# Delta inputs of a four-part kernel: scans at the end of VectorE's step, decay projected last, sums of squares in column tiles

## The reference, cut to what matters

```python
q = silu(silu(short_conv(h @ Wq, conv_q)))
k = silu(silu(short_conv(h @ Wk, conv_k)))
v = silu(short_conv(h @ Wv, conv_v))
beta, gamma = sigmoid(h @ Wb), sigmoid(h @ Wdec)
mix = sigmoid(silu(short_conv(h @ Wmix, conv_mix)) + mix_bias)
# q, k divided by sqrt(sum of squares per head + 1e-6), 4 heads of 64 columns
ema[t] = gamma[t] * ema[t-1] + (1 - gamma[t]) * v[t]      # a scan over the rows
# and, per chunk of 32 rows, the products k @ k.T that the delta rule inverts
```

## Time and profile before

| | |
|---|---|
| median of 3 runs | 1427.38 us (1426.36 to 1428.32) |
| the profiled execution's own time | 1430.96 us |
| its span (first to last instruction) | 1429.3 us |
| mean granted TensorE clock | 0.919 of full |
| busy in the span | PE 1274.9, DVE 822.0, POOL 497.4, ACT 463.4 us |
| `delta_inputs` in the trace | from about 621 to 913 us |

### The profile page before, as it was taken

The page is one execution under the profiler, slowest core; times in us unless marked ns, Lnnn a source line. Parts: engine busy times, 40 slices in busy tenths (PEclk is TensorE's granted clock), DMA queues, the critical chain, the costliest instruction groups (busy, mean ns, idle before and its releaser), DMA issues. The chain is left out here.

```text
span 1429.3 us, 36337 instructions
## 1 busy us (share of the span) xinstructions
PE 1274.9 (89%) x12853; PEld 951.0 (67%) x12854; DVE 822.0 (58%) x1882; ACT 463.4 (32%) x1085; POOL 497.4 (35%) x711
## 2 busy tenths in 40 slices
PE   6999999899999999927889787498999999889997
PEld 5888888767777777614555454387888888646564
DVE  5778888633222222238789887357566666435443
ACT  1211112132222222217667776112222222123332
POOL 3334666414511111064665642223343444210000
PEclk9999999989999999968878888559999999779999
DMA  9999910112321111121454433712643335000001
GB/s 313 351 369 341 330 44 35 36 51 100 118 64 59 59 59 59 52 77 52 141 142 128 123 89 94 195 50 74 111 108 95 95 94 149 7 1 30 30 22 37
DMA packets 219962, 156.60 MB, mean 110 GB/s; under 512 B 111744, under 2 KB 201344, under 8 KB 219840
## 3 DMA queue, kind: packets, MB, share of 16 engines
q1 hardware_dynamic: 210528, 129.51, 30.9%
q0 software_dynamic: 9312, 25.44, 5.3%
HBM read 64.47 MB, written 90.44 MB: 108 GB/s over the span
## 5 line engine op out<-in xcount | busy, mean ns | idle before, releaser
L945 PE MATMUL ps_sc<-w,a_qeo 128*128 x568 | 183.3, 466 | 0.0
L753 DVE TENSOR_TENSOR a_stm<-a_vpad,ps_sc 128x352 f32<-128x352 f32 x71 | 37.0, 521 | 177.3 <-ACT a_vpad L517 156.6
L945 PEld LDWEIGHTS ps_sc<-w,a_qeo 128*128 128x128 f32 x568 | 104.1, 193 | 46.5 <-issue 2.5
L423 POOL DMA_DIRECT2D x_slots<-a_stm x66 | 36.5, 552 | 226.1 <-issue 226.1
L1583 PE MATMUL d_pp<-d_xT,d_w_p 128*128 128x512 f32 x192 | 110.3, 721 | 1.1 <-ACT d_xT L1328 1.1
L1479 DVE SCALAR_TENSOR_TENSOR d_cout<-d_cin,d_taps,d_cout 128x512 f32<-128x512 f32 x144 | 106.2, 747 | 6.4 <-ACT d_cout L1346 3.0
L915 PE MATMUL ps_kv<-w,a_stm 128*128 x426 | 105.7, 384 | 1.2 <-DVE a_stm L746 1.2
L915 PEld LDWEIGHTS ps_kv<-w,a_stm 128*128 128x128 f32 x426 | 79.3, 190 | 30.2 <-issue 12.7
L2326 PE MATMUL g_pp<-g_xT,g_w_g 128*128 128x512 f32 x192 | 89.3, 604 | 8.3 <-ACT g_xT L2217 8.3
L1258 POOL DMA_INDIRECT got<-x_slots,d_idx x64 | 74.0, 1156 | 18.7 <-issue 16.1
L517 ACT ACTIVATE a_vpad<-ps_sc 128x352 f32<-128x352 f32 x71 | 33.0, 464 | 140.1 <-PE ps_sc L945 140.1
(11 more groups left out here) (275 smaller groups left out, 2839.8 us busy)
## 6 DMA issues: line engine op xcount, KB each, us to landing
x_slots<-a_zeros SPq DMA_DIRECT2D x32, 1024.0 KB, 10.9
rec<-d_kve SPq DMA_DIRECT2D x32, 384.0 KB, 2.9
u_kve<-rec SPq DMA_DIRECT2D x32, 384.0 KB, 3.5
a_qeo<-x_slots SPq DMA_DIRECT2D x71, 128.0 KB
x_slots<-a_stm POOLq DMA_DIRECT2D x66, 128.0 KB
rec<-d_act_out SPq DMA_DIRECT2D x32, 256.0 KB
u_qkT<-rec SPq DMA_DIRECT2D x32, 256.0 KB, 3.1
w<-in_w SPq DMA_DIRECT2D x4, 1408.0 KB, 13.9
```

Source lines behind the costliest of these rows:

```text
L753: dve.tensor_tensor(e_h[:, q, 0:HID], e_gate[:, q, :], ps_3[q], ALU.mult).then_inc(h_out, 1)
L945: mm = pe.matmul(ps, e_xT[:, q, k, :], w13[:, s, k, bass.ds(e_hidden, 1), :], start=(k == 0), stop=(k == KD - 1))
```

## The change

Three things change in `delta_inputs`.

1. `ORDER` becomes 4, 5, 2, 3, "s", 0, 1, "g0", "g1". The decay projections are the last two of the group.
2. In DVE's step the block with `d_dec_t` and the scans, and the `rows` ahead of it, go to the very end, behind conv(0) and conv(1); conv(3) comes ahead of the scales.
3. The sums of squares. Before, each block of squares was the stationary operand of a matmul (16 matmuls of 128 by 128 stationary and 8 moving columns). Now a new `sum_rows` on PE makes 4 matmuls in which the squares move (512 columns) against a stationary matrix of 32 columns, each into its own 32 partitions of a `d_ps_tok` bank; ACT copies the bank to `d_sq` (a new `sum_rows` there), and 4 matmuls with 8 moving columns pick the sums. The two `d_ps_tok` banks are therefore used 7 times per group, not 6.

The core of the diff:

```diff
-        ORDER = [4, 5, "s", 2, "g0", "g1", 3, 0, 1]
+        ORDER = [4, 5, 2, 3, "s", 0, 1, "g0", "g1"]
...
+                def sum_rows():
+                    act.wait_ge(tok_done, 7 * v + 7)
+                    act.activation(sq[:, 0, :], ps_tok[(7 * v + 6) % 2][:, :], ACT.Copy).then_inc(tok_out, 1)
...
                 if tiles:
                     tokens(5)
+                    sum_rows()
                 if here:
                     silu(u, q, 5)
                     use(7)
                     use(8)
+                    silu(u, q, 2)
                     use(9)
-                    silu(u, q, 2)
+                    silu(u, q, 3)
                     use(10)
-                    silu(u, q, 3)
...
-                if i in EARLY_ROWS_AT:
-                    rows(*EARLY_ROWS_AT[i])
-                if here:
-                    dve.wait_ge(dec_done, u + 1)
-                    ...  (d_dec_t, the two scans)
                 if here:
                     conv(2)
+                    conv(3)
                 if tiles:
                     dve.wait_ge(sums_done, v + 1)
...
                 if here:
-                    conv(3)
                     conv(0)
                     conv(1)
+                if i in EARLY_ROWS_AT:
+                    rows(*EARLY_ROWS_AT[i])
+                if here:
+                    dve.wait_ge(dec_done, u + 1)
+                    ...  (d_dec_t, the two scans)
...
+                def sum_rows():
+                    pe.wait_ge(sq_done, 4 * (v + 1))
+                    wait(pe, tok_out, 7 * v + 5)
+                    for b in range(4):
+                        mm = pe.matmul(ps_tok[(7 * v + 6) % 2][32 * b:32 * b + 32, :], sel_q[:, :], sq[:, b, :], start=True, stop=True)
+                    mm.then_inc(tok_done, 1)
+
                 def sums():
-                    pe.wait_ge(sq_done, 4 * (v + 1))
+                    pe.wait_ge(tok_out, 7 * v + 7)
                     pe.wait_ge(sm_out, v + 1)
                     for j in range(GROUP):
-                        for b in range(4):
-                            at = 64 + j * 2 * H
-                            mm = pe.matmul(ps_s[:, at:at + 2 * H], sq[:, b, j * P:(j + 1) * P], sel_q[:, b, :],
-                                           start=(b == 0), stop=(b == 3))
+                        at = 64 + j * 2 * H
+                        mm = pe.matmul(ps_s[:, at:at + 2 * H], sq[:, 0, j * P:(j + 1) * P], sel_n[:, :], start=True, stop=True)
                     mm.then_inc(sums_done, 1)
```

More of the change, by code:

```diff
@@ L1031, in load_delta_weights @@
         sp.dma_start(kept[name][:, :, :], w[of].rearrange("(k p) n -> p k n", p=P)).then_inc(loaded, 16)
-    sp.dma_start(kept["sel_q"][:, :, :], w["c_sums"]).then_inc(loaded, 16)
+    sp.dma_start(kept["sel_q"][:, :], w["c_sums"]).then_inc(loaded, 16)
+    sp.dma_start(kept["sel_n"][:, :], w["c_pick"]).then_inc(loaded, 16)
     sp.dma_start(kept["sel_d"][:, :, :], w["c_decay"]).then_inc(loaded, 16)
@@ L1039, in load_delta_weights @@
         sp.dma_start(kept["rms"][DH * e:DH * e + DH, :], w["rms_w"]).then_inc(loaded, 16)
-    return 16 * 19
+    return 16 * 20
 def gate_weights(nc, ctx):
@@ L1120, in delta_inputs @@
         sel_q = kept["sel_q"]
+        sel_n = kept["sel_n"]
         mix_b = kept["mix_b"]
@@ L1223, in step @@
                     for pair in range(2):
-                        sp.wait_ge(tok_out, 6 * u + 3 * pair + 3)
+                        sp.wait_ge(tok_out, 7 * u + 3 * pair + 3)
                         for j in (2 * pair, 2 * pair + 1):
@@ L1355, in silu @@
                         wait(act, qk_sent, 64 * (u - 1))
-                    wait(act, tok_done, 6 * (u - 1))
+                    wait(act, tok_done, 7 * (u - 1))
                     wait(act, g_done, u - 1)
@@ L1544, in step @@
                 if here:
-                    conv(3)
                     conv(0)
                     conv(1)
+                if i in EARLY_ROWS_AT:
+                    rows(*EARLY_ROWS_AT[i])
+                if here:
+                    dve.wait_ge(dec_done, u + 1)
+                    dve.wait_ge(silu_done, 6 * u + 2)
+                    dve.scalar_tensor_tensor(out=dec_t[:, :, :], in0=dec_t[:, :, :], scalar=1.0, in1=act_out[:, q, 4:6, :],
+                                             op0=ALU.subtract, op1=ALU.mult).then_inc(inp_done, 1)
+                    dve.wait_ge(inp_done, u + 1)
+                    wait(dve, tok_done, 7 * (u - 1))
+                    wait(dve, ema_done, 2 * u)
+                    for b in range(2):
+                        dve.tensor_tensor_scan(ema[:, q, b, :], dec[:, b, :], dec_t[:, b, :],
+                                               0.0 if u == 0 else ema[:, 1 - q, b, GW - 1:GW], ALU.mult, ALU.add)\
+                           .then_inc(ema_done, 1)
             pipelined(dve, NG, DEPTH, step, singly=NG)
@@ L1592, in tokens @@
                         pe.wait_ge(ema_done, 2 * (v + 1))
-                    wait(pe, tok_out, 6 * v + n - 1)
+                    wait(pe, tok_out, 7 * v + n - 1)
                     for j in range(2):
@@ L1598, in tokens @@
                             at = j * D + b * P
-                            mm = pe.transpose(ps_tok[n % 2][:, at:at + P], src, ident[:, :])
+                            mm = pe.transpose(ps_tok[(7 * v + n) % 2][:, at:at + P], src, ident[:, :])
                     mm.then_inc(tok_done, 1)
@@ L2402, in constants @@
         "c_small": sum((row == 32 * c + np.arange(2 * NH1)) & ((np.arange(2 * NH1) < NH1) | (c == HIST)) for c in range(CONV)).astype(f),
-        "c_sums": np.stack([row // DH == np.arange(2 * NH1) - (2 * b + (0 if b < 2 else 0)) for b in range(4)], 1).astype(f),
+        "c_sums": (row // DH == np.arange(32)).astype(f),
+        "c_pick": ((row // 32 == np.arange(2 * NH1) // 2) & (row % 32 == np.arange(2 * NH1) % 2)).astype(f),
         "c_decay": np.stack([(row - HIST * 32 - 2 * NH1 == 2 * n + col // DH) for n in range(KD)], 1).astype(f),
```

6 lines of the change are left out of this document (3 added, 3 removed).

## The result

The changed kernel took 1445.69 us (median of 4 runs, 1438.99 to 1448.05) beside 1427.85 us of the kernel before (4 runs, 1426.36 to 1434.95): ratio 1.0107, 95% interval 1.0059 to 1.0155. The forecast was 1442, slower. The profiled execution took 1446.63 us (span 1445.0); that of before was 1430.96 (1429.3), so 15.7 us of span are to be explained.

A forecast was written before the change was run, and what follows sets the result against it. A loop of waits through POOL, DVE, ACT and PE was to bound the stage: 0.1 + 13.6 + 7.9 + 0.1 + 10.95 + 2.55 = 35.2 us a turn against 32.3, 14.6 over five steps, so 1427.4 + 14.6 = 1442 us; range 1430 to 1458.

The forecast's parts named there:

- The ring: Loop from POOL's `d_dec` through DVE's conv(4), ACT's tanh and decay projections: 35.2 us a turn against 32.3.
- POOL's piece: On POOL, from `d_dec` start through gathers and root to the end of the `d_cin` copy: 13.6 us.
- conv(4) to d_sm_m: On DVE, from conv(4) to the end of the small op that ACT's tanh waits for: 7.9 us.
- ACT's own work: On ACT, from the tanh to the end of the last decay tanh, without waits: 10.95 us.
- ACT's waits for PE: ACT waiting for use(7) and use(8), PE's first 5.5 us at half clock: 2.55 us a turn.
- The first link to bind: DVE's conv(4) would wait for POOL's `d_cin` copy, or x_res for the last gather: 2 to 4 us a step.
- The sums: New `sum_rows` on PE, four tiles side by side: 1.0 us at full clock, 2.0 at half; 3.63 us of records removed.
- rival that they run in series: Column tiles run one behind the other, `sum_rows` 3.43 us, turn 37.8, total 1455 us; chance 0.17.
- The pauses where the tiling changes: PE draining at tiling changes: 1.0 us a turn, 5 us in total, left out of the sum, kept in the range.
- First and last steps: Steps of the stage outside the five full ones: taken as 0, bounds -3.9 and +3.9 us.
- The total: Five full steps 14.6 us longer in all, giving 1442 us against the median of 1427.4.
- rival "faster": Loop through `carried` does not bind, DVE does: five steps 149.4 us, total 1415 us; chance 0.10.

The follow-up runs named there:

- e3: Changed kernel with POOL's gathers of tiles 2 and 3, root and small writes moved ahead of `d_dec`: 1419.16 us, ratio 0.9938.
- e5: Changed kernel with only POOL's gathers of tiles 2 and 3 moved ahead of `d_dec`; root and copy of `d_cin` stay behind it: 1414.64 us, ratio 0.9922.
- e4: Changed kernel with POOL's copy of `d_cin` moved right behind `d_dec`, ahead of the gathers and root: 1442.48 us, ratio 1.0119.
- e2: Kernel before with only the new sums of squares (part 3), old order and scans: 1438.67 us, ratio 1.0079.
- e9: Changed kernel with 7 filler matmuls of 384 columns on PE ahead of `sum_rows`: 1449.08 us, ratio 1.0167.
- e1: Changed kernel with the old sums of squares and no `sum_rows` (parts 1 and 2 only): 1435.57 us, ratio 1.0041.
- e5_again: Same kernel as e5, run once more on the same chip as e12: 1416.06 us, ratio 0.9921.
- e12: Changed kernel with the old sums of squares and POOL's gathers of tiles 2 and 3 ahead of `d_dec`: 1406.00 us, ratio 0.9840.
- e6: Kernel of e3 with the old sums of squares: 1422.57 us, ratio 0.9939.

## Why the prediction was right, point by point

- **The ring** (POOL's queue behind `d_dec`, conv(4), the tanh, the decay projections): shown. e3 and e5 break it on POOL's side, and the time falls below that of before.
- **POOL's piece**: 13.6 said, 13.1 measured. **conv(4) to d_sm_m**: 7.9 and 8.0. **ACT's own work**: 10.95; the trace has 12.85 with a wait of 1.43 in it, so 11.4. **ACT's waits for PE**: 2.55 said, 1.43 measured; this is the term that was mis-sized most. Waits 1.1 too high, POOL 0.5 too high and ACT's own work 0.5 too low make the turn 34.1 and not 35.2. The walk let ACT wait for use(7) and use(8); it waited only for use(8), because the half clock ended within use(7) (2.98 us where the walk took 3.4).
- **The first link to bind**: I named conv(4)'s wait for the copy, with the last gather in brackets. It was the gather, 4.0 to 5.1 us against at most 1.1, in the first three of the five steps; in the last two, where DVE has its `rows` as well, each is about 1.3. e4 shows that the copy alone doesn't matter. Of the prediction's links this one was in the wrong order.
- **The sums**: the tiles ran side by side, 1.07 us for 8 records at full clock (e2, e9) and 1.94 at half (after), as taken (1.0 and 2.0). The rival that they run in series (3.43) is refuted. But the sum held the sums' price only inside ACT's 10.95 + 2.55, and did not say that without part 3 that piece would be 10.6 and the turn no longer than before. What the runs show: parts 1 and 2 cost 0.41% (e1, 5.9 us), and part 3 another 0.7 to 0.8% in three pairs (e2 alone, after against e1, e5_again against e12), but nothing in the fourth (e3 against e6), where the old sums lie in no gap.
- **The pauses where the tiling changes**: the Trainium skill (TensorEngine Tiling (Array Packing), Tiling Modes) would have had a drain at each change, and the prediction left it out. Use(7) follows `sum_rows` at once (in e5_again 730.20 + 1.06, then 731.20): no pause that shows. Pauses of 0.5 us at `gram` are more frequent, 6.7 us in 16 from 621 to 900 against 1.0 in 2, but e1 has 5.9 in 13 without any column tiles and e5_again 1.5 in one with them, so the new tiles don't make them. What does is open; in the changed kernel PE then stands idle 5 us ahead of `sum_rows`, which can hide them.
- **First and last steps**: taken as 0, within 3.9 either way; measured +4.0 and -3.1, which nearly cancel.
- **The total**: 14.6 said. In the five steps 8.3 came, at the stage's end 9.2. The median rose by 17.8; it agrees with the forecast partly by luck, through the 6.5 us behind the stage, of which the prediction had no step, and which I can't lay to the change. The forecast was right on sign and ring, too high by 5 us on the stage.
- **The rival "faster"** (1415, if the copy comes ahead of conv(4)): it did not happen here, but e5 and e3 bring that case about by hand, and with 1414.64, and 148.5 us for the five steps where it said 149.4, its price was right.

**What stays open**: what a full clock throughout would give in the ring; what part 3 would cost with a PSUM bank of its own; and where, in what lies behind the stage, the stretch at 1.2 GHz ends.

## What to carry to other kernels

When a wait is moved later in an engine's queue, everything behind it moves too: list it, and put what others need first (here the gathers) ahead of it. Work of a busy engine is free where it fills a gap in the ring; before it is replaced by less work, look at what the new work waits for, because a shared buffer can tie it to an engine that it used to run beside. Here the reordering and the new sums, each meant to remove a wait or work, both lost, and the same reordering with one queue put right and the third part left out is 1.6% faster.

## What was not expected of the hardware

- A gather that POOL starts 0.14 us behind the start of DVE's `d_dec_t` over 1024 columns takes 2.05 us, most others 0.95 to 1.5 (761.79 and 766.66). It is so in three turns of the changed kernel and in five of before; where the gather started 0.35 us ahead of `d_dec_t` (778.24 in before) it took 1.09. That the one lengthens the other was not tested by itself.
- Four column tiles of 512 moving columns hold PE for 1.00 us from start to start (730.20 to 731.20 in e5_again), where two records one behind the other take 0.86: nearly all of the four run at once.
